# A 64-sequence attention block with routed experts: earlier padding of the experts' rows, loads awaited on their own signals, look-ups ahead of waits

## The chip, the cores and the metric

One Trainium2 chip, one core of it. The time is device microseconds of one execution of the whole program, the median of several runs. Engines are called PE (TensorE), DVE (VectorE), ACT (ScalarE), POOL (GpSimd) and SP (SyncE, which here only issues transfers).

## What is computed

The input is x (64 sequences of 128 tokens, 128 wide) and a context (64 x 77 x 128). Four residual layers follow one another:

```python
x = x + cross_attention(latents=layernorm(x), keys_from=[ctx_1024, latents])   # 8 heads of 64, l2-normed q and k
x = x + int8_linear(layernorm(x))                                             # per-token quantization
x = x + softmax_attention_over_tokens(layernorm(x) @ We, ctx_1024) @ W2.T
t = layernorm(x)
e = argmax(t @ Wr.T + br)                                                     # one of 8 experts for each token
x = x + (relu(t @ W1[e].T + b1[e]) @ W2[e].T + b2[e])                         # 128 -> 512 -> 128
```

All four layers count here, but the change touches the last one: 8192 tokens, each sent to one of eight experts.

## The kernel before, in words

**Rounds.** The first three layers run as a software pipeline of rounds j = -1 to 74 (`rounds`, line 293), one sequence entering in each; rounds 18 to 57 are a hardware loop, the others are written out. Sequences are taken in 16 groups of four. `rho` is the place of a round in the cycle of four, `g` the group that enters; work on a group is spread over about twelve rounds. Round 64 and later (`TAIL`) take in no new sequence and only drain the pipeline.

**Routing.** When a group is through the third layer (rho 0, two groups later), DVE finds each token's expert, its place in the expert's part of a DRAM buffer `sorted_rows` (lines 876 to 896 and 973 to 991), and copies the rows, with mean, root and token number, into `stage` (`send`, line 1012). POOL writes them to `sorted_rows` with four indirect transfers a group (`scatter`, line 620). Each expert's part is as long as all tokens and one tile of 128 rows. The last group, 15, is staged in round 74.

**Tiles.** The expert layer works on tiles of 128 rows of one expert, T = 71 in all, some filled up with padding rows whose token number is out of bounds, so that their output goes nowhere. From round 64 on, three tiles stand in each round. Tiles 0 to 40 (NA = 41) hold only rows of the first twelve groups: their table (expert and first row of each tile) is made in rounds 59 to 62 from a count that PE takes in round 59 (`TOTAL_AT`, `count`, line 1353). Tiles 41 to 70 need the counts of all groups. Behind round 74 the remaining tiles of the first part run in a plain list (`REST`, k = 32 to 41), then the second part (`SECOND_PART`, k = 39 to 71).

**One tile on the engines.** `prep(k)` on DVE (line 742) prepares tile k + 2: it loads the expert's number into a register (line 746), waits, normalizes the rows (750), copies the expert's first weights (753), adds the residual and the bias (755). PE's `tile(k)` (line 1326) transposes tile k + 1 (1335), makes the hidden layer of tile k (1341) and the output of tile k - 1 (1349). ACT copies the transpose (449) and does relu (454). `finish(k)` on DVE (line 758) adds the output of tile k - 1 (768), once the store of the tile four before it has landed, and POOL stores it (`store`, line 609). Engines run their own instructions in order, so a wait of one instruction holds all behind it.

**Order in a tail round.** On DVE: prep, the window of the third layer, finish, prep, `later`, finish, prep, finish. On PE: slot_a, a tile, slot_b, a tile, slot_c, a tile, and so on. On POOL, in rho 3: centring and scaling of a group (`t_c`, lines 644 to 654) first, then a store, the inverse root (lines 674 to 686), two stores. PE transposes `t_c` in slot_c of that round (1305).

**Transfers of the rows.** SP loads tiles from `sorted_rows` (`load`, line 398), six in flight (`DEEP`), each landing on one of six semaphores `ld`; when tile k has landed, SP raises a seventh, `rows_in` (line 410), for which `prep` waits (line 748).

**The end of the first part.** Behind round 74, PE counts all groups, DVE copies the totals (`last_total`, line 846) and works out where each expert's rows end (`pad_i`). SP then writes one tile of padding rows behind each expert's last row (lines 419 to 422), from a row in SBUF, eight transfers one behind another. DVE makes the table of the second part in four pieces (`last_table`, line 855), one behind each prep of k = 32 to 35. SP waits for the table, the padding and the last scatter (lines 423 to 426) and loads tiles 41 to 70. An early transfer at line 389 also writes padding rows, 8 tiles behind all parts.

Of the kernel before, what the change touches and what calls it, by code (L numbers as in the profile page):

```python
# [9 lines left out]
I32 = mybir.dt.int32  # L10
# [39 lines left out]
def whole(nc, x_res, ctx_res, ident, w1_all, w2_all, table, sent, padded, sorted_rows, out, x, ctx, mask,  # L50
# [16 lines left out]
    with ExitStack() as stack:  # L67
# [214 lines left out]
        tile_names = ("rows_in", "w1_set", "t_set", "T_done", "t_copied", "h_done", "relu_done", "y_done", "xb_set", "fin",  # L282
# [48 lines left out]
        TOTAL_AT = 4 * (EARLY + 2) + 3  # L331
# [24 lines left out]
        def _(sp):  # L356
# [232 lines left out]
        def _(pool):  # L589
# [39 lines left out]
            def run(j, par, rho, g, inside=False):  # L629
# [14 lines left out]
                if rho == 3 and group(g - 1, inside):  # L644
# [3 lines left out]
                    pool.wait_ge(rs_ready, chain(j - 1, inside))  # L648
# [4 lines left out]
                                            rstd[:, 1 - par, 28:28 + G].unsqueeze(2).to_broadcast([P, G, D]),  # L653
# [72 lines left out]
            nc.gpsimd.memset(table["fill"][:, 0:D + 2], 0.0).then_inc(setup_p, 1)  # L726
            nc.gpsimd.memset(table["fill"][:, D + 2:D + 3].bitcast(I32), FILL).then_inc(setup_p, 1)
# [13 lines left out]
        def _(dve):  # L741
            def prep(k, part):
# [69 lines left out]
            def first_total():  # L812

                dve.wait_ge(s["tot_done"], 1)
                nc.vector.tensor_copy(table["total"][:, :], ps[:, 3, 0:E]).then_inc(s["tot_copied"], 1)

            def first_table(j):

                if j == TOTAL_AT:
                    dve.wait_ge(s["tot_copied"], 1)  # L820
# [25 lines left out]
            def last_total():  # L846

                dve.wait_ge(s["tot_done"], 2)
                nc.vector.tensor_copy(table["total"][:, :], ps[:, 3, 0:E]).then_inc(s["tot_copied"], 1)
                dve.wait_ge(s["tot_copied"], 2)  # L850
# [174 lines left out]
            def run(j, par, rho, g, inside=False):  # L1025
# [63 lines left out]
                if not inside and j == TOTAL_AT:  # L1089
                    first_total()  # L1090
# [67 lines left out]
            def setup_second():  # L1158

                dve.wait_ge(setup_p, 16)  # L1160
# [388 lines left out]
```

## Time and profile before

| what | us |
|---|---|
| median of three runs | 1051.12 (1049.69 to 1051.59) |
| the profiled execution | 1048.07 |
| its span, first to last instruction | 1046.3 |
| PE, DVE, ACT, POOL busy in the span | 979.4, 795.1, 740.3, 468.0 |
| mean granted clock of PE, share of full speed | 0.986 |
| round 64 begins, round 74 ends, second part begins (read from the timelines) | 844, 950, 977 |

Times in the profile are counted from the first instruction. In timelines a row is: start, length, engine, line, operation, output and inputs, shapes, count, and in brackets how long the engine was idle before and which instruction released it. A releaser called "issue" means that nothing in the profile was waited for, "remote" that the releaser is not known. Spans of POOL are rough, and ends of matmuls are modelled.

### The profile page before, as it was taken

How to read it: one execution, taken by the hardware profiler on the slowest of the kernel's cores; microseconds unless marked ns; L12 is line 12 of the kernel's file. 1: busy time of each engine (PE TensorE's matmuls, PEld its weight loads, DVE VectorE, ACT ScalarE, POOL GpSimd, SP SyncE). 2: the span in 40 equal slices, each digit the busy share in tenths (PEclk: the TensorE clock that was granted, in tenths of full speed). 3: DMA queues.
4: the chain of work that ended last, by engine and by line, in shares of the span. 5: the costliest groups of instructions: out<-in, count | busy, mean ns of one | idle time of the engine just before them, and what ended most of it. 6: DMA issues, size and time to landing. Idle time of an engine off the chain costs nothing.

```text
span 1046.3 us, 31979 instructions
## 1 busy us (share of the span) xinstructions
PE 979.4 (94%) x10989; PEld 861.2 (82%) x10989; DVE 795.1 (76%) x2585; ACT 740.3 (71%) x1753; POOL 468.0 (45%) x1094
## 2 busy tenths in 40 slices
PE   2799999999999999999999999999998988887997
PEld 1688888888888888888888888888887878877897
DVE  3566778888888888888888888888888867755553
ACT  1688877777777777777777877777776655554564
POOL 3333323353545353535353535343434335664455
PEclk9999999999999999999999999999999998998999
DMA  5743000000000000000000000000000032011310
GB/s 133 213 115 61 3 2 2 2 12 2 12 1 10 0 10 0 10 0 10 0 10 0 10 3 8 3 7 5 5 7 6 5 70 74 30 34 50 87 50 22
DMA packets 45124, 28.38 MB, mean 27 GB/s; under 512 B 11039, under 2 KB 41698, under 8 KB 45042
## 3 DMA queue, kind: packets, MB, share of 16 engines
q1 hardware_dynamic: 39586, 17.79, 6.8%
q0 software_dynamic: 4320, 8.50, 2.5%
q10 hardware_dynamic: 1136, 1.05, 0.3%
q8 instruction: 46, 0.75, 0.3%
q14 instruction: 36, 0.29, 0.1%
HBM read 17.75 MB, written 10.02 MB: 27 GB/s over the span
## 4 chain that ended last, share of the span: by engine, by line
PE 80%; ACT 5%; DVE 4%; issue 4%; SPq 3%; POOL 2%; another core or an unknown queue 1%; DMA 1%; DVEq 0%; POOLq 0%; ACTq 0%
PE ps L1421 13%; PE ps L1384 10%; PE ps L1362 8%; PE ps L1188 7%; PE ps L1190 7%; PE ps L1189 7%; PE ps L1460 7%; PE ps L1349 4%; PE ps L1341 4%; PE ps L1446 3%; PE ps L1440 2%; SPq L399 2%; SPq L400 1%; PE ps L1216 1%; PE ps L1231 1%
## 5 line engine op out<-in xcount | busy, mean ns | idle before, releaser
L1080 DVE TENSOR_REDUCE sumsq<-qk_hat 128x8 f32<-128x512 f32 x192 | 124.0, 678 | 44.9 <-ACT qk_hat L491 44.6
L1421 PE MATMUL ps<-qT_all,kT_all 64*128 64x128 f32 x2048 | 149.6, 286 | 1.8 <-ACT w_all L500 1.2
L1384 PE MATMUL ps<-v_sb,prob 128*64 128x65 f32 x4096 | 144.5, 224 | 6.2 <-ACT qq_t L541 2.4
L1384 PEld LDWEIGHTS ps<-v_sb,prob 128*64 128x64 f32 x4096 | 129.0, 138 | 25.3 <-issue 13.3
L550 ACT ACTIVATE prob<-ps,neg_shift 128x512 f32<-128x512 f32 x128 | 88.6, 692 | 79.4 <-PE ps L1421 79.3
L1103 DVE TENSOR_TENSOR qk_hat<-ps,rstd 128x512 f32<-128x512 f32 x192 | 120.6, 684 | 26.9 <-POOL rstd L686 26.3
L491 ACT ACTIVATE qk_hat<-ps 128x512 f32<-128x512 f32 x192 | 113.3, 598 | 39.1 <-PE ps L1190 28.9
L1421 PEld LDWEIGHTS ps<-qT_all,kT_all 64*128 64x128 f32 x2048 | 125.0, 188 | 19.2 <-ACT prob L550 13.1
L1188 PE MATMUL ps<-w_hi,xc_hi 128*128 128x512 f32 x320 | 138.3, 432 | 0.8 <-DVE mask_bias L1155 0.8
L679 POOL TENSOR_TENSOR rs_t<-rs_y 128x32 f32<-128x32 f32 x73 | 17.8, 243 | 259.7 <-ACT rs_y L528 259.7
L1190 PE MATMUL ps<-w_hi,xc_lo 128*128 128x512 f32 x320 | 126.6, 396 | 0.0
L1189 PE MATMUL ps<-w_lo,xc_hi 128*128 128x512 f32 x320 | 126.0, 394 | 0.0
L614 POOL DMA_INDIRECT out_dram<-o_n,x_res x71 | 78.7, 1108 | 73.3 <-DVE o_n L768 41.7
L478 ACT ACTIVATE v_sb<-ps 128x512 f32<-128x512 f32 x128 | 76.5, 599 | 40.3 <-PE ps L1190 34.7
L1362 PE MATMUL ps<-ident,qk_hat 128*128 128x128 f32 x768 | 95.8, 275 | 4.1 <-DVE qk_hat L1103 4.1
L1362 PEld LDWEIGHTS ps<-ident,qk_hat 128*128 128x128 f32 x768 | 87.1, 143 | 4.7 <-DVE qk_hat L1103 4.5
L1349 PE MATMUL ps<-w_all,kT_all 128*128 x568 | 79.8, 286 | 5.4 <-ACT kT_all L454 4.6
L550 ACT ACTIVATE prob<-ps,mask_now 128x512 f32<-128x512 f32 x128 | 82.5, 714 | 0.5 <-PE ps L1421 0.3
L1349 PEld LDWEIGHTS ps<-w_all,kT_all 128*128 128x128 f32 x568 | 73.2, 202 | 6.6 <-issue 6.1
L625 POOL DMA_INDIRECT sorted_rows<-stage,idx x64 | 70.7, 1105 | 17.4 <-issue 15.5
L1460 PE MATMUL ps<-wo_sb,o_t 128*128 128x128 f32 x512 | 74.1, 288 | 1.7 <-ACT o_t L572 0.7
L1460 PEld LDWEIGHTS ps<-wo_sb,o_t 128*128 128x128 f32 x512 | 61.9, 191 | 13.0 <-ACT o_t L572 11.2
(227 smaller groups left out, 2142.1 us busy)
## 6 DMA issues: line engine op xcount, KB each, us to landing
x_res<-sorted_rows SPq DMA_DIRECT2D x71, 65.5 KB
w_all<-in_L_ffn_W_dram SPq DMA_DIRECT2D x16, 256.0 KB, 5.9
x_res<-in_x_dram SPq DMA_DIRECT2D x5, 768.0 KB
ctx_res<-in_ctx_dram SPq DMA_DIRECT2D x5, 462.0 KB
out_dram<-o_n,x_res POOLq DMA_INDIRECT x71
sorted_rows<-stage,idx POOLq DMA_INDIRECT x64
sorted_rows<-fill SPq DMA_DIRECT2D x1, 524.0 KB, 5.2
sorted_rows<-table_fill SPq DMA_DIRECT2D x8, 65.5 KB
```

Source lines behind the costliest of these rows:

```text
L491: nc.scalar.activation(sq[:, n * INNER:(n + 1) * INNER], ps_qk[:, n, :], ACT.Square).then_inc(sq_done, 1)
L550: nc.scalar.activation(prob[:, n // 2, n % 2 * INNER:(n % 2 + 1) * INNER], ps_s[n], ACT.Exp, bias=(mask_now[:, par:par + 1] if n > 1 else ...
L1080: nc.vector.reduce_sum(sumsq[:, n * H:(n + 1) * H], sq[:, n * INNER:(n + 1) * INNER].rearrange("p (h d) -> p h d", d=DH), AX).then_inc(ss_ ...
L1103: nc.vector.tensor_tensor(qk_hat[:, n * INNER:(n + 1) * INNER].rearrange("p (h d) -> p h d", d=DH), ps_qk[:, n, :].rearrange("p (h d) -> p ...
L1188: nc.tensor.matmul(dst, tok_hi, w_hi[:, w:w + INNER], start=True, stop=False)
L1189: nc.tensor.matmul(dst, tok_hi, w_lo[:, w:w + INNER], start=False, stop=False)
L1190: return nc.tensor.matmul(dst, tok_lo, w_hi[:, w:w + INNER], start=False, stop=True)
L1349: last = nc.tensor.matmul(ps_y[(k - 1) % 2], h_t[:, (k - 1) % 2, c, :], flat(w2_all[:, bass.ds(e, 1), c * P:(c + 1) * P]), start=c == 0, s ...
L1362: last = nc.tensor.transpose(ps_qk[:, n, t * P:(t + 1) * P], qk_hat[:, n * INNER + t * P:n * INNER + (t + 1) * P], ident[:, :])
L1384: last = nc.tensor.matmul(dst[half:half + DH, :], prob[:, kt, at + half:at + half + DH], v_sb[:, 1 - par, kt, h, :], start=kt == 0, stop=k ...
L1421: last = nc.tensor.matmul(ps_s[2 * kt + half][:, cols], k_t[rows, kt, cols], q_t[rows, cols], start=True, stop=True)
L1460: last = nc.tensor.matmul(ps_o, o_t[:, t * P:(t + 1) * P], wo_sb[:, t, :], start=t == 0, stop=t == PAIRS - 1)
```

## The change

1. **Padding.** A second count is taken in round 71 (`PAD_AT`), in which groups 0 to 14 are counted. SP then writes G + 1 = 5 tiles of padding rows behind each expert's last row so far, 640 rows in one transfer from the row `fill`, and waits for each landing before the next. POOL's scatter of group 15 waits for all eight, since its rows overwrite padding. The third count stands behind round 74, as the second did, without pad starts. The row `table["fill"]` and two fills of POOL at the start go.
2. **Loads.** `rows_in` goes: DVE waits for the landing on `ld` itself.
3. **Look-ups.** The expert's number is loaded by `look_up`, placed behind the previous `prep` and ahead of the waits of `window` or `finish`.
4. **t_c.** In the tail, `t_c` is made in rho 2, behind the inverse root and ahead of the second store, not at the start of rho 3.
5. **Table.** `last_table` runs two pieces behind each of the preps of k = 32 and 33.

```diff
-        TOTAL_AT = 4 * (EARLY + 2) + 3
+        TOTAL_AT, PAD_AT = 4 * (EARLY + 2) + 3, 4 * (NG + 1) + 3
...
-                for k in range(lo, lo + DEEP):
-                    if k >= 2 * DEEP and k - DEEP < lo:
+                for k in range(lo, hi):
+                    if k >= DEEP:
                         sp.wait_ge(ld[k % DEEP], 16 * (k // DEEP))
                     load(k)
-                for k in range(lo, hi):
-                    sp.wait_ge(ld[k % DEEP], 16 * (k // DEEP + 1))
-                    sp.sem_inc(se["rows_in"], 1)
-                    if k + DEEP < hi:
-                        load(k + DEEP)
...
-                row = sp.value_load(table["pad_i"][0:1, e:e + 1], min_val=0, max_val=(E - 1) * PART + B * P)
-                sp.dma_start(sorted_rows[bass.ds(row, P), :], table["fill"][:, :]).then_inc(padded, 16)
+                row = sp.value_load(table["pad_i"][0:1, e:e + 1], min_val=0, max_val=(E - 1) * PART + (B - G) * P)
+                sp.dma_start(sorted_rows[bass.ds(row, (G + 1) * P), :].rearrange("(t p) w -> p t w", p=P),
+                             fill[:, :, :].to_broadcast([P, G + 1, D + 3])).then_inc(padded, 16)
+                sp.wait_ge(padded, 16 * (e + 1))
             sp.wait_ge(s["routed"], TABLE_R)
-            sp.wait_ge(padded, 16 * E)
...
+                if rho == 3 and group(g - 1, inside) and not tail(j, inside):
+                    centred(j - 1, g)
                 if tail(j, inside):
                     store(tile_no(j, 0), 0)
...
+                if rho == 2 and tail(j, inside) and group(g - 1, inside):
+                    centred(j, g)
                 if tail(j, inside):
                     store(tile_no(j, 1), 0)
                     if g - 2 == NG - 1 and rho == 0:
+                        pool.wait_ge(padded, 16 * E)
                         scatter(g - 2, (0, 1), inside)
...
+            def look_up(k, part):
+                if has_tile(k + 2, part):
+                    number[k + 2] = dve.value_load(texp_i[0:1, k + 2:k + 3], min_val=0, max_val=E - 1)
+
             def prep(k, part):
                 if has_tile(k + 2, part):
-                    n = (k + 2) % 4
-                    e = dve.value_load(texp_i[0:1, k + 2:k + 3], min_val=0, max_val=E - 1)
+                    n, e = (k + 2) % 4, number[k + 2]
                     past(dve, "T_done", k - 2)
-                    past(dve, "rows_in", k + 2)
+                    dve.wait_ge(ld[(k + 2) % DEEP], 16 * ((k + 2) // DEEP + 1))
...
+                        look_up(-2, 0)
+                        look_up(-1, 0)
                         dve.wait_ge(sim_done, 4 * B)
                         prep(-2, 0)
                     prep(tile_no(j, 0), 0)
+                    look_up(tile_no(j, 1), 0)
                 window(j, par, rho, g, inside)
                 if tail(j, inside):
                     finish(tile_no(j, 0), 0)
                     prep(tile_no(j, 1), 0)
+                    look_up(tile_no(j, 2), 0)
                     if rho != 0:
                         later(j, par, rho, g, inside)
                     finish(tile_no(j, 1), 0)
                     prep(tile_no(j, 2), 0)
+                    look_up(tile_no(j + 1, 0), 0)
...
                 if not inside and j == TOTAL_AT:
-                    first_total()
+                    copy_total(1)
+                if not inside and j == PAD_AT:
+                    copy_total(2)
+                    pad_starts()
...
-            last_total()
+            copy_total(3)
             for k in REST:
                 prep(k, 0)
-                last_table(k - REST[0])
+                look_up(k + 1, 0)
+                if k < REST[2]:
+                    for piece in (0, 1):
+                        last_table(2 * (k - REST[0]) + piece)
                 finish(k, 0)
+            look_up(SECOND_PART[0], 1)
             for k in SECOND_PART:
                 prep(k, 1)
+                look_up(k + 1, 1)
                 finish(k, 1)
...
-                if not inside and j == TOTAL_AT:
+                if not inside and j in (TOTAL_AT, PAD_AT):
                     after(pe, "pr_done", g - 1, inside)
-                    after(pe, "before_done", EARLY - 1, inside)
+                    after(pe, "before_done", g - 2, inside)
                     count()
-                    pe.wait_ge(s["tot_copied"], 1)
+                    pe.wait_ge(s["tot_copied"], 1 if j == TOTAL_AT else 2)
```

`copy_total(n)` waits for the n-th count, copies it and waits for the copy; `pad_starts` is the rest of `last_total` (lines 851 and 852).

## Rows read from the trace of the kernel before

**Rows 1.** The page, part 1: busy time of the engines.

```profile
PE 979.4 (94%) x10989; PEld 861.2 (82%) x10989; DVE 795.1 (76%) x2585; ACT 740.3 (71%) x1753; POOL 468.0 (45%) x1094
```

**Rows 2.** By stretch: length, busy PE, PEld, DVE, ACT, POOL, clock, DMA.

```profile
...
984.40:1046.30 61.90, 54.75 (x483) 54.09 (x483) 31.80 (x108) 36.85 (x140) 33.57 (x30) 0.98 0.16 44
...
```

**Rows 3.** Timeline of DVE, round 71: start, length, line, [idle before, releaser].

```profile
...
922.18 0.35 DVE L750 TENSOR_SCALAR xc_hat<-x_res 128x128 f32<-128x128 f32 x1 [0.45 <-issue]
...
922.78 0.28 DVE L755 TENSOR_TENSOR qT_all<-x_res,w_all 128x128 f32<-128x128 f32 x1
...
```

**Rows 4.** Timeline of PE, round 71: the start of tile 22.

```profile
...
920.74 0.33 PE L1335 MATMUL ps<-ident,xc_hat 128*128 128x128 f32 x1
...
```

**Rows 5.** DVE's sequencer, line 746: its loads of expert numbers (ns min/median/max).

```profile
...
L746 DVEq TENSOR_LOAD <-table_texp_i x71: 297/304/550, 845.2 to 1033.2; - x71
...
```

**Rows 6.** The chain that ended last, 900 to 935: start, length, what.

```profile
...
914.86 0.19 DVEq L746
...
930.39 0.19 DVEq L746
...
```

**Rows 7.** Timeline of DVE behind the last round.

```profile
...
950.30 0.28 DVE L768 TENSOR_TENSOR o_n<-ps,qT_all 128x128 f32<-128x128 f32 x1
...
950.88 0.17 DVE L852 CAST table_pad_i<-table_pad_f 128x8 int32<-128x8 f32 x1
...
965.91 0.19 DVE L809 SCALAR_TENSOR_TENSOR table_trow_i<-table_row_b,table_trow 128x30 int32<-128x30 f32 x1
...
978.09 0.35 DVE L750 TENSOR_SCALAR xc_hat<-x_res 128x128 f32<-128x128 f32 x1 [0.43 <-SPq L410]
...
988.45 0.29 DVE L768 TENSOR_TENSOR o_n<-ps,qT_all 128x128 f32<-128x128 f32 x1 [0.28 <-PE ps L1349]
...
990.35 0.29 DVE L768 TENSOR_TENSOR o_n<-ps,qT_all 128x128 f32<-128x128 f32 x1 [0.28 <-DVE qT_all L755]
...
```

**Rows 8.** Timeline of PE: the transposes of t_c, rounds 69 and 73.

```profile
...
903.36 0.66 PE L1305 MATMUL ps<-ident,t_c 128*128 128x128 f32 x4 [0.74 <-POOL t_c L652]
...
936.83 0.66 PE L1305 MATMUL ps<-ident,t_c 128*128 128x128 f32 x4 [1.65 <-POOL t_c L652]
...
```

**Rows 9.** Timeline of POOL, rounds 72 and 73.

```profile
...
931.29 0.32 POOL L686 TENSOR_TENSOR rstd<-rs_t 128x32 f32<-128x32 f32 x1
...
934.38 1.07 POOL L649 TENSOR_TENSOR t_c<-x_res,stat_c 128x512 f32<-128x512 f32 x1
...
```

**Rows 10.** By stretch, after two idle spells of PE (columns as in rows 2).

```profile
...
938.50:945.00 6.50, 6.50 (x33) 6.50 (x32) 2.22 (x10) 2.00 (x8) 2.01 (x2) 0.50 0.10 30
...
961.00:965.50 4.50, 4.41 (x20) 4.42 (x21) 3.24 (x12) 1.81 (x8) 2.30 (x2) 0.50 0.26 75
...
```

**Rows 11.** SP's queue: eight paddings, first load behind them, last padding, its wait.

```profile
...
951.82 12.03 SPq L422 DMA_DIRECT2D sorted_rows<-table_fill  x8
966.84 35.53 SPq L400 DMA_DIRECT2D x_res<-sorted_rows  x30
...
963.51 0.33 SPq L422 DMA_DIRECT2D sorted_rows<-table_fill  x1
...
L406 SPq EVENT_SEMAPHORE  x1: 1132/1132/1132, 964.0 to 964.0; - x1
...
```

**Rows 12.** The page, part 6: the padding of 1,024 rows, us to landing.

```profile
sorted_rows<-fill SPq DMA_DIRECT2D x1, 524.0 KB, 5.2
```

**Rows 13.** Timeline of POOL behind the last round: scatters and stores.

```profile
...
951.21 0.96 POOL L625 DMA_INDIRECT sorted_rows<-stage,idx  x1 [1.22 <-DVE idx L1023]
...
957.70 0.99 POOL L614 DMA_INDIRECT out_dram<-o_n,x_res  x1 [0.30 <-issue]
...
```

**Rows 14.** Timeline of PE behind the last round.

```profile
...
956.16 0.33 PE L1335 MATMUL ps<-ident,xc_hat 128*128 128x128 f32 x1 [1.55 <-issue]
...
961.09 2.07 PE L1349 MATMUL ps<-w_all,kT_all 128*128 x8 [3.71 <-ACT kT_all L454]
...
```

**Rows 15.** Timeline of ACT at the second of these.

```profile
...
959.81 1.14 ACT L454 ACTIVATE kT_all<-ps,qk_hat 128x128 f32<-128x128 f32 x4 [4.78 <-remote]
...
```

More of the change, by code:

```diff
@@ L281, in whole @@
         s = {n: sem("m_" + n) for n in names}
-        tile_names = ("rows_in", "w1_set", "t_set", "T_done", "t_copied", "h_done", "relu_done", "y_done", "xb_set", "fin",
+        tile_names = ("w1_set", "t_set", "T_done", "t_copied", "h_done", "relu_done", "y_done", "xb_set", "fin",
                       "out_sent0", "out_sent1", "out_sent2", "out_sent3")
@@ L643, in run, with centred @@
                     scatter(g - 2, (2 * rho - 2, 2 * rho - 1), inside)
-                if rho == 3 and group(g - 1, inside):
+                def centred(j, g):
                     after(pool, "tcT_done", g - 2, inside)
                     after(pool, "x3_done", g - 1, inside)
-                    pool.wait_ge(rs_ready, chain(j - 1, inside))
+                    pool.wait_ge(rs_ready, chain(j, inside))
                     nc.gpsimd.tensor_tensor(t_c[:, :, :], grp(x_res, g - 1),
@@ L652, in run @@
                     nc.gpsimd.tensor_tensor(t_c[:, :, :], t_c[:, :, :],
-                                            rstd[:, 1 - par, 28:28 + G].unsqueeze(2).to_broadcast([P, G, D]),
+                                            rstd[:, j % 2 if tail(j, inside) else 1 - par, 28:28 + G].unsqueeze(2).to_broadcast([P, G, D]),
                                             ALU.mult).then_inc(s["tc_done"], 1)
+                if rho == 3 and group(g - 1, inside) and not tail(j, inside):
+                    centred(j - 1, g)
                 if tail(j, inside):
@@ L725, in _ @@
             nc.gpsimd.iota(table["base_i"][:, :], pattern=[[PART, E]], base=0, channel_multiplier=0).then_inc(setup_p, 1)
-            nc.gpsimd.memset(table["fill"][:, 0:D + 2], 0.0).then_inc(setup_p, 1)
-            nc.gpsimd.memset(table["fill"][:, D + 2:D + 3].bitcast(I32), FILL).then_inc(setup_p, 1)
             nc.gpsimd.memset(before[:, :], 0.0).then_inc(setup_p, 1)
@@ L741, in _ @@
         def _(dve):
+            number = {}
+            def look_up(k, part):
+                if has_tile(k + 2, part):
+                    number[k + 2] = dve.value_load(texp_i[0:1, k + 2:k + 3], min_val=0, max_val=E - 1)
             def prep(k, part):
                 if has_tile(k + 2, part):
-                    n = (k + 2) % 4
-                    e = dve.value_load(texp_i[0:1, k + 2:k + 3], min_val=0, max_val=E - 1)
+                    n, e = (k + 2) % 4, number[k + 2]
                     past(dve, "T_done", k - 2)
-                    past(dve, "rows_in", k + 2)
+                    dve.wait_ge(ld[(k + 2) % DEEP], 16 * ((k + 2) // DEEP + 1))
                     row = rows[:, k + 2, :]
@@ L810, in tiles_listed, with copy_total @@
                                                     ALU.mult, ALU.add))
-            def first_total():
-                dve.wait_ge(s["tot_done"], 1)
+            def copy_total(n):
+                dve.wait_ge(s["tot_done"], n)
                 nc.vector.tensor_copy(table["total"][:, :], ps[:, 3, 0:E]).then_inc(s["tot_copied"], 1)
+                dve.wait_ge(s["tot_copied"], n)
             def first_table(j):
                 if j == TOTAL_AT:
-                    dve.wait_ge(s["tot_copied"], 1)
                     step(nc.vector.tensor_copy(table["iota_f"][:, :], table["iota_i"][:, 0:T]))
@@ L844, in _, with pad_starts @@
             last_end = []
[L846 to L850, printed above, removed]
+            def pad_starts():
                 step(nc.vector.tensor_tensor(table["pad_f"][:, :], table["base_f"][:, :], table["total"][:, :], ALU.add))
@@ L1158, in setup_second @@
             def setup_second():
-                dve.wait_ge(setup_p, 16)
+                dve.wait_ge(setup_p, 14)
                 nc.vector.tensor_copy(ident_bf[:, :], ident[:, :])
@@ L1509, in layers @@
         shapes = dict(total=[E], iota_f=[tiles], base_f=[E], ntile=[E], ntile_a=[E], tend=[2, E], end_a=[E], skip=[E],
-                      skip_a=[E], jump=[E], pad_f=[E], row_b=[tiles - first], ended=[first, E], texp=[first], trow=[first],
-                      fill=[D + 3])
+                      skip_a=[E], jump=[E], pad_f=[E], row_b=[tiles - first], ended=[first, E], texp=[first], trow=[first])
         table = {name: sb("table_" + name, [P] + shape) for name, shape in shapes.items()}
```

## Prediction, before the changed kernel was run

> **What bounds the kernel now.** I read part 1 of the page first: PE is busy 94% of the span, DVE 76%, POOL 45% [rows 1]. Only time at which PE stands idle or runs at half clock can be won. The change touches nothing before round 59 but two fills of POOL at the start (POOL is free there for most of its time, cost 0), and in round 59 only the place of a wait, so I looked at the tail, from round 64 (about 843 us) on. The stretch behind 984 us is PE's own: 54.75 of 61.90 us busy, and what is left is the wind-down [rows 2]. The winnable time lies from 843 to 984, in spots where PE waits for DVE, POOL or ACT.
>
> **The added wait in round 71.** PE counts, then waits until DVE has copied the total. In DVE's program the copy stands behind the preparation of tile 24, whose last instruction ran from 922.78 to 923.06 [rows 3]. With the look-up hidden (0.35 less) and a copy like the 0.17 us of its neighbour at line 852, PE goes on at about 923.0; it now begins that tile at 920.74 [rows 4]. Nothing else is queued for PE, and behind it on DVE stand finish(22) and the group's residual add, which need PE's results. Cost: 923.0 - 920.74 = **2.2 us**, all on the path. Bounds: 1.5 (DVE comes earlier) and 3.
>
> **The look-ups.** A load of an expert's number takes DVE's sequencer 0.30 us [rows 5], and with what follows it DVE stands idle 0.45 us before line 750 [rows 3] when it comes out of a wait. Ahead of the wait this is free, about 0.1 stays: 0.35 us each. Of the rounds' 33 preparations only those on the chain pay: from 900 to 935 the chain passes this load five times, first at 914.86, last at 930.39 [rows 6]. One of them I counted above, at most two more lie on the path before 900: 6 x 0.35 = **2.1 us** won. Bounds 1 and 4. In the rest and in the second part, where PE is the bound, I cost them at nothing, and at the joint too: look_up(39) stands right before prep(39), so the 0.43 us idle there stay [rows 7].
>
> **Centring and scaling a round earlier.** PE waits 0.74 us in round 69 and 1.65 us in round 73 for t_c [rows 8]. The changed kernel computes it as soon as the root is there, 931.61 instead of 934.38 [rows 9], 2.8 us earlier, which covers both: **2.4 us** won. What becomes late is a pair of stores, by some 2.3 us; a store is waited for only four tiles later (7.6 us at 1.90 us a tile [rows 7]).
>
> **The clock.** Behind the 1.65 us of idling PE ran 6.5 us at 0.50 of full speed [rows 10], 1.2 instead of 2.4 GHz. That cost half of 6.5, 3.3 us. The new idling of 2.2 us in round 71 is longer than the one that goes, so I move this price two rounds ahead and count **0**; bounds 3.3 either way.
>
> **The padding.** Now eight transfers of 128 rows are issued back to back in 12 us, and then loads begin, at 966.84, held by the table (965.91), not by padding [rows 7, 11]. The first load is needed at 978.09 [rows 7], eleven microseconds later; so direct waits on landings and an earlier table win nothing there: **0**. The new transfers carry 640 rows and each waits for the one before. From the end of line 852 (951.05) to the issue takes 0.77 us [rows 7, 11]. Landing is not shown for 640 rows: 128 rows took from 963.51 to 965.10, 1.6 us; 1,024 rows took 5.2 [rows 11, 12]. The straight line between gives 3.7, but sixteen small loads were issued behind the large one, so I take 2.8, nearer the lone one. The Trainium skill ("DMA: Bandwidth & Descriptors", Anatomy of one DMA) has about 2.0 us plus bytes at 436 GB/s; that is 2.15 for 128 rows, where the trace has 1.6, and by its estimate of 2.8 for 640 the sum would be the same, but every serial transfer pays the fixed part, which speaks against this form. A cycle is 0.77 + 2.8 = 3.6 us, eight are 29. They start at about 923.4, where two short steps follow the copy, and end at **X = 952.2**. Bounds: at 2.0 for landing X = 946; at 5.2, X = 971.
>
> **Who waits for X.** POOL waits for all eight before the last group's scatter, with four scatters and the stores of tiles 30 and 31 behind. They run 1.30 us apart [rows 13]; store 31 is the sixth, issued at X + 6.5, landed about 1.6 us later: X + 8.1. DVE needs it in finish(36), five tiles of 1.90 behind finish(31) at 950.30 [rows 7], thus 959.8, and by the terms above 2.3 earlier, 957.5; PE can bear about 1 us more. PE stands idle for X - 950.4 = **1.8 us**. Loads of the second part need the scatters landed, X + 8 = 960, against a need at about 975: hidden.
>
> **What goes behind the last round.** There PE now idles 1.55 us before 956.16 and 3.71 us before 961.09 [rows 14], and then runs 4.5 us at 0.50 [rows 10]. The second is ACT coming 4.78 us late with relu, for a releaser that the profile does not name [rows 15]. It lies within the eight padding transfers and six DMAs of POOL one behind another. With the padding gone from there, and two steps of DVE with it, I let both idle spells go, 5.3 us, and set the 1.8 us in their place: **3.5 us** won; the half clock I leave. Bounds: 0 won before the hold is subtracted if the stall is POOL's own; 7.5 if the half clock goes too and there is no hold.
>
> **Sum.** -2.2 + 2.1 + 2.4 + 0 + 0 + 3.5 = 5.8 us won. The profiled execution took 1048.07 us (span 1046.3); the median of the three runs is 1051.12, 3.05 above it. I subtract from the median: **1045.3 us**. A measurement of this kernel can tell about 0.2%, 2.1 us, from no change: faster is below 1049.0, slower above 1053.2.
>
> **Rivals.**
> - *Stall is POOL's own* (0.20). ACT, DVE and SP all fall behind while POOL starts one indirect DMA after another; in the changed kernel the same six stand in a row. Then nothing is won behind the last round, and 1.8 of hold hides in the stall: 5.8 - 3.5 = 2.3 won, 1048.8. For it: ACT's unnamed releaser [rows 15]; against: the longest stall is where padding ran too.
> - *One more half-clock phase* (0.13). The new idling cools PE in round 71, and round 73 is not spared: 1045.3 + 3.3 = 1048.6; with part of the first rival it ends within 0.2% of before.
> - *Padding too slow* (0.17, the one on the other side). If landing takes 4.3 us or more, as on the straight line plus traffic of POOL's stores on the same DMA engines, a cycle is 5.1, X = 964, and PE idles 13.6 us where 5.3 go: -2.2 + 2.1 + 2.4 - 8.3 = -6.0, 1057.1. It decides from the point where X passes 960: 9.7 us of hold make the sum -2.1, that is a landing of 3.8 us.
> - *No half clock, no hold* (0.10). Both spells and their slow stretches go: 5.8 + 1.8 + 2.2 (half of 4.5) = 9.8 won, 1041.3; with the look-ups at their bound, 1039.4.
> - *It does not do what it says* (0.02): loads and look-ups are hidden and padding never was the wait; 1051.
>
> My forecast has 0.38 (1043 to 1048). The range of 8 in 10 goes from 1039.5, the case without hold, to 1055, half of the slow case; its width is that of the landing time, a single number times eight. Below 1049.0 lie the forecast, the last but one and somewhat over half of the first two rivals: 0.38 + 0.10 + 0.14 = 0.62. Within: 0.19 of these and 0.02, less the slow ends of both: 0.19. Above: 0.17 and those ends, 0.19.
>
> **What would show it.** Right: in round 71 PE idle about 2.2 us before its tile 22; line 1305 without a wait; eight padding transfers some 3.6 us apart between 923 and 952; POOL's first scatter of the last group just behind the last landing; ACT's relu without a wait of several us near 957. Wrong: a padding cycle over 4.6 us, with finish waiting for stores and PE idle behind the last round (slower); the stall of ACT still there without any padding near it (the first rival); two stretches at 0.50 between 920 and 950 (the second); look-ups that leave 0.45 us before line 750 would take the 2.1 us away.

## Result and profile after

| | before | after |
|---|---|---|
| median, us | 1050.82 (6 runs) | 1054.01 (6 runs, 1052.95 to 1055.34) |
| profiled execution, its span | 1048.07, 1046.3 | 1053.26, 1051.5 |

The ratio after to before is 1.0032 [1.0019, 1.0045]: 0.3% slower. The time lies near the upper end of the forecast's range (1039.5 to 1055), on the other side of the kernel before. The two profiled executions lie 5.2 us apart, the medians 3.2. PE's busy time is what it was [rows 1]; what grew is the time in which it stands.

Part 1 of the page of the changed kernel, and then stretches of its trace (columns as in rows 2):

```profile
PE 979.4 (93%) x10990; PEld 860.8 (82%) x10990; DVE 791.9 (75%) x2586; ACT 739.7 (70%) x1753; POOL 459.9 (44%) x1092
```

```profile
922.00:931.00 9.00, 7.82 (x46) 7.83 (x47) 3.90 (x19) 2.96 (x12) 3.09 (x4) 0.62 0.30 89
931.00:950.50 19.50, 16.86 (x147) 16.15 (x147) 10.99 (x40) 10.60 (x41) 11.81 (x16) 1.00 0.34 98
...
966.00:977.40 11.40, 4.58 (x24) 4.59 (x25) 2.17 (x8) 3.19 (x13) 4.90 (x6) 0.70 0.27 70
984.40:1051.50 67.10, 58.86 (x510) 57.33 (x509) 33.27 (x119) 39.86 (x150) 30.35 (x31) 0.98 0.16 42
```

Two places lost it: round 71 (clock 0.62 of full speed between 922 and 931) and the time behind the last round, where from 966 to 977 PE works 4.58 of 11.4 us. The half clock of round 73 [rows 10] is gone: 1.00 from 931 to 950.5. The same points of DVE's program in both traces show where the time went. `finish(21)` begins at 921.45 before and 921.23 after; `finish(22)`, the first behind the new wait, at 923.04 and 927.20, so 4.2 us later; `finish(31)`, the last of round 74, at 950.30 and 952.30, 2.0 us later. Then come `finish(34)` and `finish(38)`, before:

```profile
963.30 0.29 DVE L768 TENSOR_TENSOR o_n<-ps,qT_all 128x128 f32<-128x128 f32 x1 [0.72 <-PE ps L1349]
...
972.11 0.29 DVE L768 TENSOR_TENSOR o_n<-ps,qT_all 128x128 f32<-128x128 f32 x1 [0.27 <-DVE qT_all L755]
```

and after:

```profile
960.29 0.29 DVE L772 TENSOR_TENSOR o_n<-ps,qT_all 128x128 f32<-128x128 f32 x1
...
977.82 0.29 DVE L772 TENSOR_TENSOR o_n<-ps,qT_all 128x128 f32<-128x128 f32 x1 [1.71 <-PE ps L1363]
```

So the changed kernel won 5.0 us from `finish(31)` to `finish(34)`, where it led by 3.0, and lost 8.7 in the next four tiles. (The same points in the two traces of group 1048, see below, give 4.9 won and 8.4 lost.)

PE in the changed kernel: the count of round 71, what follows it, t_c in round 73, and the tiles behind the last round.

```profile
919.78 0.17 PE L1368 MATMUL ps<-before,ones_pp 128*128 128x8 bf16 x1
...
923.18 0.47 PE L1349 MATMUL ps<-ident,xc_hat 128*128 128x128 f32 x1 [3.23 <-DVE table_total L819]
...
940.48 0.60 PE L1319 MATMUL ps<-ident,t_c 128*128 128x128 f32 x4
...
972.82 2.07 PE L1363 MATMUL ps<-w_all,kT_all 128*128 x8 [6.95 <-ACT kT_all L450]
```

The tile that began at 920.74 before [rows 4] begins at 923.18, after 3.23 us of idling. The transposes of t_c, which waited 1.65 us [rows 8], wait for nothing. (POOL's four stores behind t_c now follow one another from 939.80, and DVE waits 3.93 us at 945.79 for a releaser that is not named; the trace before has no such wait there.) And the 3.71 us behind the last round [rows 14] have become 6.95.

SP's queue, the line of the paddings (ns min/median/max, first and last issue), and then POOL:

```profile
923.65 31.15 SPq L417 DMA_DIRECT2D sorted_rows<-fill  x8
968.63 5.58 SPq L400 DMA_DIRECT2D x_res<-sorted_rows  x5
```

```profile
L417 SPq DMA_DIRECT2D sorted_rows<-fill x8: 16/372/716, 923.6 to 954.4; - x8
```

```profile
950.55 0.99 POOL L610 DMA_INDIRECT out_dram<-o_n,x_res  x1 [0.30 <-issue]
958.56 0.96 POOL L621 DMA_INDIRECT sorted_rows<-stage,idx  x1 [7.03 <-DMA sorted_rows<-fill]
...
968.91 0.97 POOL L610 DMA_INDIRECT out_dram<-o_n,x_res  x1 [0.30 <-issue]
```

The eight paddings are issued from 923.6 to 954.4, seven intervals of 4.40 us, and the last has landed by 958.5. POOL stands 7.03 us for it, and then issues nine indirect DMAs in a row, the first at 958.56 and the last at 968.91 (before it was six [rows 13]). DVE and ACT behind that:

```profile
963.54 0.29 DVE L772 TENSOR_TENSOR o_n<-ps,qT_all 128x128 f32<-128x128 f32 x1 [2.17 <-DMA out_dram<-o_n,x_res]
...
971.73 0.29 DVE L772 TENSOR_TENSOR o_n<-ps,qT_all 128x128 f32<-128x128 f32 x1 [7.11 <-remote]
```

```profile
971.54 1.14 ACT L450 ACTIVATE kT_all<-ps,qk_hat 128x128 f32<-128x128 f32 x4 [6.88 <-remote]
```

DVE waits 2.17 us for a store that landed late, since it stood behind the hold. Then ACT waits 6.88 us for a releaser that the profile does not name, as in rows 15, and goes on 1.7 us after POOL's last DMA of the row has ended (969.88).

### The profile page after: what moved, and what is told of

It is laid out like the page before. It is cut to its first block, busy times and chain, and to the rows that moved or that the text cites. A ratio compares the mean times of both kernels' runs of the same rounds, so it can differ in the third digit from the quotient of the medians.

```text
span 1051.5 us, 31911 instructions
## 1 busy us (share of the span) xinstructions
PE 979.4 (93%) x10990; PEld 860.8 (82%) x10990; DVE 791.9 (75%) x2586; ACT 739.7 (70%) x1753; POOL 459.9 (44%) x1092
## 4 chain that ended last, share of the span: by engine, by line
PE 83%; ACT 5%; DVE 5%; issue 3%; POOL 1%; another core or an unknown queue 1%; DMA 1%; DVEq 0%; POOLq 0%; ACTq 0%; SPq 0%
PE ps L1435 13%; PE ps L1398 11%; PE ps L1376 8%; PE ps L1202 7%; PE ps L1204 7%; PE ps L1203 7%; PE ps L1474 7%; PE ps L1355 5%; PE ps L1363 5%; PE ps L1460 3%; PE ps L1454 2%; PE ps L1245 1%; PE ps L1239 1%; PE ps L1230 1%; PE ps L1265 1%
## 5 line engine op out<-in xcount | busy, mean ns | idle before, releaser
L610 POOL DMA_INDIRECT out_dram<-o_n,x_res x71 | 71.1, 1001 | 75.9 <-DVE o_n L772 48.9
L772 DVE TENSOR_TENSOR o_n<-ps,qT_all 128x128 f32<-128x128 f32 x71 | 20.6, 290 | 69.9 <-PE ps L1363 43.2
## 6 DMA issues: line engine op xcount, KB each, us to landing
x_res<-sorted_rows SPq DMA_DIRECT2D x71, 65.5 KB
sorted_rows<-fill SPq DMA_DIRECT2D x8, 327.5 KB
```

## The experiments

Kernels that ran together ("this call" in the expectations, a group here) share a chip and the runs of the kernel before. A group is named by what the kernel before took in it: 1052 (1051.85 us), 1040 (1040.24), 1048 (1047.64), 1038 (1037.88) and 1047 (1047.04). So ratios are compared, and times within a group alone. The two differ where the kernel before itself drifted: in group 1040 it ran from 1035.59 to 1042.96 us. A size in us that is given with a ratio there is the ratio's. "Old padding" is the changed kernel with the padding of the kernel before.

### Taking the new padding out again

```diff
-                             fill[:, :, :].to_broadcast([P, G + 1, D + 3])).then_inc(padded, 16)
-                sp.wait_ge(padded, 16 * (e + 1))
+                sp.dma_start(sorted_rows[bass.ds(row, P), :], fill[:, 0, :]).then_inc(padded, 16)
...
-                        pool.wait_ge(padded, 16 * E)
...
-                if not inside and j in (TOTAL_AT, PAD_AT):
+                if not inside and j == TOTAL_AT:
```

with the end positions computed behind round 74 again. It ran in the groups 1052, 1048 and 1047.

> The changed kernel with the padding of the kernel before (behind the last round, eight transfers of one tile each, no count and no wait of TensorE in round 71); the look-ups, the table's order, the loads' own signals and t_c a round earlier stay. Theory (the padding's part is what loses): these other parts win 3 to 4.5 us against the kernel before, 1047 us, with the half clock of round 73 gone. Rival (the other parts are worth nothing): 1050 to 1051 us, as the kernel before.

> The first experiment's kernel once more (the changed kernel with the padding of the kernel before), on the chip of this call, beside the changed kernel. Theory: 5 to 6 us faster than the kernel before and 8 to 9 us faster than the changed kernel, on any chip. Rival (its 0.5% belonged to the chip of the first call): within 0.2% of the kernel before here.

> The changed kernel with the old padding, without gaps, on the chip of this call. Theory (gaps did nothing where there is no stall): 0.994 to 0.995 of the kernel before on a chip without remote stalls, 0.995 to 0.999 on one with them. Rival (the gaps were what won on the chips without stalls): 0.997 or more there.

Measured against the kernel before: 1045.99 us, 0.9950 [0.9932, 0.9968]; 1047.26 us, 0.9986 [0.9969, 1.0002]; 1045.14 us, 0.9984 [0.9971, 0.9997]. So the other parts of the change do win, by 0.1 to 0.5% (in group 1048 the interval reaches 1.0002), and the new padding, with its count and its wait, is what loses. The first theory's size of 5 to 6 us on any chip does not hold: the gain was 5.9, 0.4 and 1.9 us by the medians.

### The parts alone

Three kernels start from the kernel before: one with the look-ups alone, one with t_c a round earlier alone, and one with only the count of round 71 and its wait:

```diff
-                if not inside and j == TOTAL_AT:
+                if not inside and j in (TOTAL_AT, PAD_AT):
                     after(pe, "pr_done", g - 1, inside)
-                    after(pe, "before_done", EARLY - 1, inside)
+                    after(pe, "before_done", g - 2, inside)
                     count()
-                    pe.wait_ge(s["tot_copied"], 1)
+                    pe.wait_ge(s["tot_copied"], 1 if j == TOTAL_AT else 2)
```

> The kernel before with the look-ups of the expert numbers alone moved ahead of VectorE's waits. The four parts that are left when the new padding is taken out of the change won 5.9 us together. Theory (forecast's term): the look-ups won 2.1 us of it, 1048.7 us here. Rival (they are hidden behind the stalls): under 1 us. Second rival (they are most of it, since every tile of the second part has one): 4 us or more.

> The kernel before with t_c of rounds 71 and 75 moved alone to the round before. Theory (forecast's term): TensorE waits 0.74 and 1.65 us less, and without the gap of 1.65 us the half clock of round 73 doesn't come: 2.4 us, or up to 3.5 with the clock: 1047.3 to 1048.4 us. Rival (the two additions of GpSimd hold the tile's store instead): no gain, 1050 us or more.

> The kernel before with the count of round 71, its copy and TensorE's wait for it added; the padding stays where it was, so that nobody uses this count. Theory (this wait is a loss of its own): TensorE stands 3 us at 920 us and its clock halves behind it, 3 to 6 us slower, 1054 to 1057 us. Rival (only the padding's traffic and the hold lose): within 1 us of the kernel before.

Measured, in group 1040: look-ups 0.9980 [0.9961, 0.9999], 2.1 us of 1040.24 (0.1 to 4.1); t_c 0.9983 [0.9966, 1.0001], 1.8 us, so by itself not quite told from nothing; the count 1.0055 [1.0028, 1.0083], 5.7 us slower (2.9 to 8.6), though nobody reads that count. The medians (1036.29, 1037.23 and 1043.37) would say 3.9 and 3.0 us faster and 3.1 slower, so the signs hold and the sizes are rough. In its trace PE, then stretches:

```profile
920.52 0.17 PE L1357 MATMUL ps<-before,ones_pp 128*128 128x8 bf16 x1
923.20 0.32 PE L1338 MATMUL ps<-ident,xc_hat 128*128 128x128 f32 x1 [2.51 <-DVE table_total L1093]
```

```profile
920.60:923.20 2.60, 0.09 (x3) 0.01 (x1) 1.25 (x5) 0.99 (x4) 1.38 (x2) 1.00 0.08 25
923.20:929.50 6.30, 6.30 (x41) 6.26 (x42) 2.34 (x8) 2.21 (x8) 1.42 (x2) 0.73 0.03 10
```

The idling is 2.51 us; behind it the clock is 0.73 on average for 6.3 us, some 1.7 us more. Together 4.2 us, of 5.7 by the ratio and 3.1 by the medians.

The half clock does not follow every such spell. The kernel with the look-ups alone stood 2.50 us before t_c in round 73 and kept 1.00 behind it. So did the kernel before in another execution (group 1048), behind 1.47 us, where [rows 10] has 0.50:

```profile
936.65 0.66 PE L1318 MATMUL ps<-ident,t_c 128*128 128x128 f32 x4 [2.50 <-POOL t_c L652]
```

```profile
936.60:943.00 6.40, 6.35 (x55) 6.13 (x56) 3.05 (x14) 3.49 (x12) 2.97 (x3) 1.00 0.10 31
```

```profile
939.80:946.00 6.20, 6.19 (x53) 5.93 (x54) 3.73 (x18) 3.49 (x12) 3.27 (x3) 1.00 0.10 32
```

### The padding's waits, and where PE waits

One kernel is the changed one without `sp.wait_ge(padded, 16 * (e + 1))`, in groups 1052 and 1047. The other, in group 1052, has in addition PE's wait behind tile 22:

```diff
-                    pe.wait_ge(s["tot_copied"], 1 if j == TOTAL_AT else 2)
+                    if j == TOTAL_AT:
+                        pe.wait_ge(s["tot_copied"], 1)
                 if tail(j, inside):
                     tile(tile_no(j, 2), 0)
+                if not inside and j == PAD_AT:
+                    pe.wait_ge(s["tot_copied"], 2)
```

> The changed kernel without SyncE's wait behind each padding transfer. Theory (the hold of GpSimd until 958 us and the nine indirect DMAs behind it cost what the change won): the eight transfers are issued at SyncE's pace and have landed before 945 us, GpSimd waits for nothing before the last group's scatter, at most six indirect DMAs come back to back, and the time is 4 us under the changed kernel, 1050 us. Rival (TensorE's wait in round 71 and its clock are the whole loss): the hold goes but the time stays at 1053 to 1054 us. Second rival (the transfers, now all at once, crowd the DMA engines): round 72 to 74 get longer and the time is 1055 us or more.

> The changed kernel without SyncE's waits between the padding transfers, on the chip of this call. Theory (wait in round 71 and hold each cost about half): on a chip without remote stalls the ratio to the kernel before is near 1.000, 6 us from either neighbour; on one with them 0.998 to 1.000, as in the first call. Rival (the hold is nearly all of it): 0.995 or less. Second rival (the wait in round 71 and the transfers' traffic are nearly all): 1.004 or more.

> As the kernel without the waits behind each padding transfer, and TensorE's wait for the copied counts in round 71 stands behind the work of tile 22 instead of ahead of it. Theory (wait and hold both count): TensorE has no idle time of 3 us at 920 us and keeps its clock, 3 us less than with the wait ahead: 1047 us. Rival (the wait only moves behind tile 22, since VectorE copies the counts where it did): the idle time comes back in another place and the time is that of the kernel with the wait ahead within 1 us.

Measured: 1050.56 us, 0.9988 [0.9971, 1.0006], and 1046.70 us, 1.0004 [0.9987, 1.0021], without the waits; 1049.47 us, 0.9975 [0.9959, 0.9991], with PE's wait later too. Old padding in the same groups stood at 0.9950 and 0.9984. In the trace of group 1052 SP issues the eight in 10.3 us and POOL waits for none of them; what stays is round 71:

```profile
924.56 10.29 SPq L417 DMA_DIRECT2D sorted_rows<-fill  x8
```

```profile
924.10 0.47 PE L1348 MATMUL ps<-ident,xc_hat 128*128 128x128 f32 x1 [3.27 <-DVE table_total L818]
```

The changed kernel stood at 1.0032 and 1.0029, though in other groups. So taking the waits out brings back some 0.25 to 0.45%, across groups, and what is left, PE's wait in round 71 and the transfers' traffic together, costs the other 0.2 to 0.4%; these two were not separated. The later wait cost PE nothing in its place, as the theory had it, but it brought 1.1 us and not 3, and the two intervals overlap. (Its traced execution, 1052.33 us, is 2.9 above its median; it lay 4 us behind the two others of its group already at `finish(21)`, ahead of round 71's wait, with PE's clock at 0.84 from 900 to 922.) In that kernel the transfers of 2.6 MB, now all at once, fill the DMA engines (share 0.77 from 922 to 950.5, against 0.09 with the old padding), and a store of a tile lands late. Stretches, and DVE at the place:

```profile
922.00:950.50 28.50, 21.93 (x183) 20.52 (x182) 13.47 (x50) 15.87 (x61) 15.30 (x20) 0.99 0.77 124
```

```profile
949.73 0.29 DVE L771 TENSOR_TENSOR o_n<-ps,qT_all 128x128 f32<-128x128 f32 x1 [6.00 <-DMA out_dram<-o_n,x_res]
```

PE stood 2.12 us behind it. That the traffic made this store late is the likeliest reading; it was not separated from the order of POOL's work.

### The stall behind POOL's indirect DMAs

```diff
+            def gap():
+                nc.gpsimd.memset(gap_tile[:, 0:512], 0.0).then_inc(gap_done, 1)
+                gaps[0] += 1
+                pool.wait_ge(gap_done, gaps[0])
...
+                    gap()
                     nc.gpsimd.indirect_dma_start(
```

> The changed kernel with a memset of 512 columns on GpSimd, and a wait for its end, ahead of each indirect DMA of the second part's rows and of the last group. Theory (ScalarE and VectorE see signals late while GpSimd issues indirect DMAs back to back): with gaps they go on within 0.5 us of what they wait for, the 7 us hold of ScalarE at 964 to 971 us is cut by 3 us or more, and the time is 1050 to 1052 us in spite of some 0.6 us more on GpSimd for each DMA. Rival (the hold is only the late landing of the padding, or the traffic of the transfers): the stalls stay as long and GpSimd is later: 1055 to 1058 us.

The edit puts a gap ahead of every store of the tail, also in the rounds: 75 memsets from 856.9 us on, more than the expectation says.

Measured: 1083.39 us, 1.0299 [1.0272, 1.0326], above both expectations. ACT's and DVE's long remote waits are gone (one of 1.8 us is left in the whole trace, where ACT's longest in the three others of group 1052 were 3.4 to 5.6), but a gap costs 1.35 us and not 0.6: the memset's 0.54 us and 0.8 until POOL sees its own signal.

```profile
L610 POOL MEMSET gap_tile<- x75: 519/544/792, 856.9 to 1075.5; 128x512 f32 x75
```

A store then takes POOL about 2.3 us where PE makes a tile in 1.90, and POOL is the bound of the second part: PE works 70.04 of its last 96 us.

> The changed kernel with the padding of the kernel before, as in the first experiment, and in the last round alone a memset of one column with a wait for its end ahead of each of the last group's four indirect DMAs and of the store between them. Theory (signals of TensorE come late while GpSimd issues six indirect DMAs back to back): ScalarE's stall of 5.6 us behind the last round shrinks below 3 us and the time falls by 1 to 3 us under 1046.0. Rival (the stall has another cause and the gaps only make GpSimd later): the stall stays and the time is 1046 to 1049 us.

> The kernel with the old padding and short waited memsets between the last round's indirect DMAs once more, on the chip of this call. Theory (a burst makes the stall on a chip that has such stalls): where the other traces of this call show remote waits, the wait of 5.5 us behind the last round is under 3 us here and the time is 0.5% or more under the kernel before. Rival (gaps do nothing): the wait of 5 us or more is still there.

Short gaps (one column) in the last round alone, with the old padding: 1032.43 us, 0.9944 [0.9923, 0.9964], and 1031.81 us, 0.9940 [0.9925, 0.9954]. But both fell in groups (1040 and 1038) in which no trace shows a long remote wait, so they say nothing of the gaps. Nor is a short gap much of one: behind an indirect DMA the next begins 0.40 us after the last one's end, where back to back it is 0.30.

```profile
944.05 0.96 POOL L631 DMA_INDIRECT sorted_rows<-stage,idx  x1 [0.60 <-POOL gap_tile L609]
945.01 0.12 POOL L609 MEMSET gap_tile<- 128x1 f32 x1
945.41 0.96 POOL L631 DMA_INDIRECT sorted_rows<-stage,idx  x1 [0.28 <-POOL gap_tile L609]
```

The kernel with the look-ups alone is of group 1040. POOL issued eleven indirect DMAs there between 947.51 and 961.36, and ACT's relu in the middle of them:

```profile
953.66 1.14 ACT L454 ACTIVATE kT_all<-ps,w_more 128x128 f32<-128x128 f32 x4 [0.59 <-PE ps L1354]
955.56 1.14 ACT L454 ACTIVATE kT_all<-ps,qk_hat 128x128 f32<-128x128 f32 x4 [0.59 <-PE ps L1354]
```

Nothing is late. So a burst alone does not make the stall. In group 1048 four such DMAs were added to the old-padding kernel, in the middle of the second part:

```diff
+                    for i in range(G):
+                        nc.gpsimd.indirect_dma_start(
+                            out=twin, out_offset=bass.IndirectOffsetOnAxis(ap=idx[:, i:i + 1], axis=0),
+                            in_=stage[:, i, :], in_offset=None).then_inc(twin_sent, 16)
```

> The kernel before, unchanged, for its trace on this chip. The traces so far fall in two kinds: with stalls of 2 to 6 us in which ScalarE and VectorE wait for something that the profile calls remote (kernel before at 1050 to 1052 us), and without any (kernel before at 1040 us), also where GpSimd issued seven to eleven indirect DMAs back to back. Theory (the stalls belong to the chip or to the execution, not to the length of the burst): a kernel before at 1040 us shows none of them, one at 1050 us shows 2 or more. Rival (the length of the burst decides): the stall at 951 to 959 us is there on any chip.

> The changed kernel with the old padding, and four more indirect DMAs back to back on GpSimd in the middle of the second part, to a tensor that nobody reads (5.1 us of GpSimd). Theory (a burst alone makes the remote stall): ScalarE or VectorE shows a remote wait of 2 us or more there. Rival (it needs this chip or other traffic): no remote wait there; VectorE waits for its output buffer at most, as GpSimd is late by 5 us.

The kernel before took 1048.52 us there, with one wait of 4.8 us of ACT and three of DVE of up to 3.3, all remote. The added burst (1051.64 us) made new ones, where there was none. ACT:

```profile
1005.99 1.14 ACT L454 ACTIVATE kT_all<-ps,w_more 128x128 f32<-128x128 f32 x4 [3.29 <-remote]
...
1010.31 0.28 ACT L449 ACTIVATE xc_t<-ps 128x128 f32<-128x128 f32 x1 [3.17 <-remote]
```

This is one execution; the old-padding kernel of the same group has no remote wait of 1 us behind 960. So in a group of this kind four added DMAs are enough, without any padding near them. Whether it is their coming one behind another or their traffic was not separated. The same four DMAs with short gaps, and memsets in their place, ran in group 1038:

> The kernel with the old padding and the four added indirect DMAs in the middle of the second part, each now behind a memset of one column whose end GpSimd waits for. Theory (back to back is what matters): no remote wait over 1 us at that place, though GpSimd is busy there for longer. Rival (the four added DMAs' work or traffic matters, however spaced): remote waits of 2 us or more as without the gaps.

> The kernel with the old padding and, in place of the four added indirect DMAs, four memsets of 512 columns with a wait for the end of each (about 5 us of GpSimd's time by the kernel with long gaps). Theory (it is the DMA instruction, not GpSimd being late): no remote wait there, VectorE waits for its output buffer alone. Rival (any 5 us of lateness on GpSimd does it): a remote wait of 2 us or more.

1034.30 and 1032.51 us, no remote wait in either; but that group is of the other kind, so the theory's rival is not tested by them. What makes a group the one kind or the other stays open. The record gives groups 1052 and 1038 the same chip number, so the number does not decide it. They divide cleanly: long remote waits at 1047, 1048 and 1052 us for the kernel before, none at 1038 and 1040.

### The changed kernel again

> The changed kernel, unchanged, on the chip of this call. Theory (TensorE's wait in round 71 costs some 5 us and the held scatter the rest, which the look-ups and t_c pay back with 4 to 6 us): 2 to 4 us slower than the kernel before on any chip, with or without the remote stalls. Rival (the remote stalls behind the burst of nine DMAs were the loss): on a chip without them the changed kernel is as fast as the kernel before or up to 4 us faster.

> The changed kernel once more, for the kind of this call's chip. Theory: 0.2 to 0.4% slower than the kernel before where remote waits show, and on a chip without them 0.1% slower to 0.3% faster, since there GpSimd's burst of nine holds nobody. Rival (TensorE's wait in round 71 and the held scatter are the whole loss): 0.2 to 0.5% slower on either kind.

With remote waits about: 1051.00 us, 1.0029 [1.0014, 1.0044], as the first time. Without any: 1044.32 us, 1.0062 [1.0044, 1.0080]. So the changed kernel loses without the stall too. The second expectation's rival had this right, though 0.6% is above its 0.5; both theories had it less slow there. In group 1038, the quiet one, its own losses stand bare, and they are larger: 12.5 us above old padding with short gaps (1031.81), where group 1048 had 3.7 (1051.00 against 1047.26). The quiet trace, POOL, DVE and PE behind the last round:

```profile
944.04 0.97 POOL L610 DMA_INDIRECT out_dram<-o_n,x_res  x1 [0.87 <-DVE o_n L772]
956.96 0.96 POOL L621 DMA_INDIRECT sorted_rows<-stage,idx  x1 [11.94 <-DMA sorted_rows<-fill]
```

```profile
961.77 0.29 DVE L772 TENSOR_TENSOR o_n<-ps,qT_all 128x128 f32<-128x128 f32 x1 [7.69 <-DMA out_dram<-o_n,x_res]
...
966.87 0.29 DVE L772 TENSOR_TENSOR o_n<-ps,qT_all 128x128 f32<-128x128 f32 x1 [4.01 <-DMA out_dram<-o_n,x_res]
```

```profile
962.38 0.47 PE L1349 MATMUL ps<-ident,xc_hat 128*128 128x128 f32 x1 [5.96 <-DVE xc_hat L754]
```

The mechanism is that of "Who waits for X" with every link named: padding, scatter, the stores behind it, DVE's output buffer, PE. The first to wait is one tile sooner than forecast: `finish(35)` at 961.77, for the third DMA of the row (tile 30's store), then `finish(36)` at 966.87 for the sixth (tile 31's). That store of POOL at 944.04 is at 941.83 in the quiet old-padding trace, and the spans differ by 10.5 us (1042.7 and 1032.2): 2.2 us were lost before the last round, in round 71, and 8.3 behind it, where only the hold stands. In the three traces of group 1040 that start from the kernel before, PE had no idle spell over 0.8 us in that place, so in such a group there was next to nothing there to win.

## Why the prediction was wrong

**Right.** The look-ups: 2.1 us predicted, 2.1 measured, but within 0.1 to 4.1 (and the chain passes the load a sixth time before 935, at 931.22). t_c: 2.4 predicted, 1.8 measured within -0.1 to 3.5, and the wait before it is gone. PE resumes in round 71 at 923.18, where 923.0 was predicted, which is partly luck: DVE's copy ended at 922.51, 0.4 sooner than forecast, and PE went on 0.67 us behind it, where I had 0.1. The wait is 3.23 us and not 2.2 mainly because PE was there 0.8 us sooner (the matmuls ahead of it begin at 918.79 for 919.55): what had been gained up to that point was idled away at once. In group 1038 it is 2.15. The half clock moved from round 73 to round 71 in these two traces. Counting it as 0 was fair for them and luck beyond them, since the kernel before ran round 73 at full clock in group 1048; it hid what the wait costs by itself, 5.7 us (2.9 to 8.6) in the isolated run.

**The step that failed is the padding's landing time.** I had two rows for it and a straight line between them that gave 3.7 us, and took 2.8, "nearer the lone one". A cycle of 0.77 + 2.8 = 3.6 was to end at X = 952.2. The measured cycle is 4.40 us, less 0.77 a landing of 3.6, and X is 958.5 (957.0 in group 1038). The straight line was right; the small loads behind the large transfer, for which I discounted it, were no reason to leave it. (The Trainium skill's form, as the prediction quotes it, gives 2.8 as well; its section is on transfers that POOL issues, these are SP's, and the measured 3.6 decides.) An error of 0.8 us, eight times, is the 6.3 us between 952.2 and 958.5: the hold of X - 950.4 becomes 8.1 us instead of 1.8. Put into the sum, this alone makes 2.3 + 5.3 - 8.1 = -0.5, about 1051.6 by the forecast's reckoning: nothing is won. The rival "padding too slow" had the mechanism, at a landing of 4.3.

**The second failed step is what stands behind the last round**, "I let both idle spells go" with 1.8 us in their place. The spells did go where they were, 5.0 us from `finish(31)` to `finish(34)` for a forecast of 5.3. What came in their place by `finish(38)` is 8.7 us and not 1.8. The hold's form had two times in it, and both were off: X, and the end of round 74, forecast at 948.0 (950.30 less 2.3) and measured at 952.30. With both put right it gives X + 8.1 - (952.30 + 9.5 + 1) = 3.8 us here, with the forecast's five tiles of 1.90 and 1 us that PE can bear; with 956.96 and 945.33 it gives 9.2 in group 1038, where 8.3 were lost. So in the first trace, by this estimate, under half of the 8.7 is the hold. The rest lies with ACT's wait of 6.88 us for an unnamed releaser, which was 4.78 before: it moved with POOL's row of DMAs, nine where six had been. The rival that the stall is POOL's own had this right, for groups that have the stall: it stayed with the old padding too (ACT 5.61, 5.53 and 4.78 us in the three groups), and the added DMAs make it elsewhere. How the 8.7 us divides between hold and stall was not measured by itself.

**The loads' own signals and the earlier table** were set at nothing and not tried alone. In group 1040 the look-ups and t_c won 2.1 and 1.8 us and all parts but the padding 5.8 (with the short gaps), so 1.9 us would be left for them, with an interval of several us: open. That the earlier table costs nothing is doubtful: in both traces with short gaps PE stands 1.80 us for DVE's `prep` right behind the last two pieces of the table (951.37 and 951.16), where the traces with the table as before have at most 0.8.

**The version that beats both** is the changed kernel with the old padding: below the kernel before in every group (0.9950, 0.9944, 0.9986, 0.9940, 0.9984; the second and fourth with short gaps; the third's interval reaches 1.0002), and 3.7 and 12.5 us under the changed kernel in the two groups that had both.

## What to carry over

A chain of transfers that each wait for the last multiplies the error in one landing time by its length; interpolate in bytes, and compute where the sum crosses the first consumer before deciding which end of a range to take. Work moved off a place that looks crowded is paid for where its result is needed: here the padding had landed at 965.10, thirteen microseconds before the first tile behind it was needed (978.09), and came to stand before four scatters, five stores and an output buffer of four tiles. And a wait put on the bound engine costs the idling, in some executions the clock behind it as well, and eats what was gained ahead of it.

## What the runs showed of the hardware

- While POOL issues four or more indirect DMAs some 0.3 us apart, ACT and DVE can stand 2 to 7 us for a releaser that the profile cannot name. How much differs: six in a row brought 4.78 us in the kernel before and 1.86 in the one without waits in group 1047. It depends on the group: absent in the two in which the same kernel is about 1% faster (1038 and 1040 against 1047 to 1052 us), even behind eleven DMAs in a row.
- A wait of POOL for its own memset of 512 columns takes 0.8 us from the memset's end to the next DMA, more than the 0.54 us of the memset. Behind memsets of one column that followed a DMA at once it was 0.28 us in three places and 0.80 in one (group 1038).
- PE's clock fell to 0.62 (changed kernel) and 0.73 (count alone) on average over the 6 to 9 us behind idle spells of 3.23 and 2.51 us; in the changed kernel it was back at 1.00 from 931 on, 8 us behind the spell's end. Behind spells of 2.50 us (look-ups alone) and 1.47 us (kernel before, group 1048) it stayed at 1.00, and behind 1.65 us in the first trace of the kernel before it was 0.50.
- Transfers from SBUF to DRAM issued by SP, in rows of 524 bytes: 65.5 KB alone landed in 1.6 us, 327.5 KB one at a time in 3.6 (cycle 4.40 less 0.77), 524 KB in 4.8 to 5.9 over the traces.
- PE went on 0.67 us after DVE's copy of the counts had ended, in three traces (923.18 behind 922.51, 921.11 behind 920.44, 923.20 behind 922.52).
